# A style-modulated 1-D network as one convolution per sample: three of four samples by shared products instead of two

## The reference, cut to what matters

```
s = style @ mw.T + mb                       # per sample and input channel
weight = SCALE * w * s[:, None, :, None]
demod = rsqrt(sum(weight * weight, axis=(2, 3)) + EPS)
weight = weight * demod[:, :, None, None]   # per sample
out = x
for i, typ in enumerate(('same','upsample','same','downsample')):
    out = layer_i(out)                      # conv (and blur) with that sample's weight
return x + out
```

## Time and profile before

| | us |
|---|---|
| median of 3 runs (lowest to highest) | 675.08 (674.23 to 676.02) |
| the profiled execution | 674.02 |
| its span | 672.2 |
| TensorE busy | 660.9 |
| VectorE, GpSimd, ScalarE busy | 436.3, 366.1, 311.8 |

### The profile page before, as it was taken

How to read it: one execution, slowest core, us unless ns; L and a number is a source line. 1 busy time by engine, 2 the same in 40 slices (tenths; PEclk the granted TensorE clock), 3 DMA queues, 4 the chain that set the end, 5 groups by cost and what they waited for, 6 DMA issues and landing times.

```text
span 672.2 us, 12153 instructions
## 1 busy us (share of the span) xinstructions
PE 660.9 (98%) x4478; PEld 615.9 (92%) x4478; DVE 436.3 (65%) x648; ACT 311.8 (46%) x494; POOL 366.1 (54%) x387
## 2 busy tenths in 40 slices
PE   8998999999999999999999999999999999999987
PEld 7887999999999999999999999999999999999986
DVE  5996666867666665586675665665767766556551
ACT  4335454543544453544454454454454454455441
POOL 2447556566656556646556655546665555665410
PEclk9999999999999999999999999999999999999999
DMA  7238776567776667867657877657877666887763
GB/s 255 61 91 213 182 181 159 157 185 199 187 178 153 178 181 185 210 152 176 172 157 196 208 184 164 167 164 181 202 190 178 140 181 171 209 197 192 154 157 130
DMA packets 130603, 117.20 MB, mean 174 GB/s; under 512 B 6064, under 2 KB 97264, under 8 KB 130544
## 3 DMA queue, kind: packets, MB, share of 16 engines
q1 hardware_dynamic: 130176, 116.17, 68.7%
q10 hardware_dynamic: 368, 0.25, 0.2%
HBM read 36.51 MB, written 33.75 MB: 105 GB/s over the span
## 4 chain that ended last, share of the span: by engine, by line
PE 94%; DVE 4%; issue 1%; ACT 1%; POOL 0%; DVEq 0%; ACTq 0%; POOLq 0%
PE po L175 17%; PE po L176 17%; PE po L177 17%; PE pg L175 8%; PE pg L177 8%; PE pg L176 8%; PE pg L180 4%; PE pg L181 4%; PE pm L177 3%; PE pm L175 3%; PE pm L176 3%; PE pe L399 1%; PE pe L392 1%; PE pg L408 0%; PE pe L402 0%
## 5 line engine op out<-in xcount | busy, mean ns | idle before, releaser
L175 PE MATMUL po<-xh,W 128*128 128x256 f32 (+1 forms) x640 | 217.7, 340 | 2.8 <-DVE T L742 1.8
L176 PE MATMUL po<-xl,W 128*128 128x256 f32 (+1 forms) x640 | 217.0, 339 | 0.0
L177 PE MATMUL po<-xh,W 128*128 128x256 f32 (+1 forms) x640 | 216.8, 339 | 0.0
L177 PEld LDWEIGHTS po<-xh,W 128*128 128x128 f32 x640 | 125.6, 196 | 12.3
L175 PEld LDWEIGHTS po<-xh,W 128*128 128x128 f32 x640 | 125.0, 195 | 12.9 <-issue 3.3
L176 PEld LDWEIGHTS po<-xl,W 128*128 128x128 f32 x640 | 125.5, 196 | 9.9
L742 DVE SCALAR_TENSOR_TENSOR T<-po,DD,M 128x512 f32<-128x512 f32 x64 | 48.0, 750 | 97.1 <-PE po L177 64.3
L667 POOL TENSOR_TENSOR Q2l<-Q2f,Q2h 128x512 fp32r<-128x512 f32 x30 | 71.6, 2386 | 68.5 <-ACT Q2h L552 68.5
L733 DVE TENSOR_TENSOR xl<-X,xh 128x1032 fp32r<-128x1032 f32 x64 | 96.3, 1505 | 2.9 <-ACT xh L513 2.9
L513 ACT CAST xh<-X 128x1032 fp32r<-128x1032 f32 x64 | 80.9, 1265 | 37.2 <-PE po L177 36.1
L768 DVE TENSOR_TENSOR Wf<-pg,S 128x512 f32<-128x512 f32 x64 | 44.2, 691 | 77.2 <-PE pg L177 57.6
(11 more groups left out here) (174 smaller groups left out, 1483.3 us busy)
## 6 DMA issues: line engine op xcount, KB each, us to landing
X<-in_xin SPq DMA_DIRECT2D x64, 516.0 KB, 4.4
out<-T SPq DMA_DIRECT2D x64, 512.0 KB, 3.7
W<-W SPq DMA_DIRECT2D x93, 256.0 KB, 4.3
W<-W SPq DMA_DIRECT2D x31, 384.0 KB, 5.6
V<-V SPq DMA_DIRECT2D x32, 128.0 KB, 5.2
V<-W SPq DMA_DIRECT2D x32, 64.0 KB, 3.6
V<-Vx SPq DMA_DIRECT2D x32, 64.0 KB, 3.0
E<-in_ed SPq DMA_DIRECT2D x1, 768.0 KB, 7.4
```

Source lines behind the costliest of these rows:

```text
L175: eng.matmul(o, wh_, rh, start=first, stop=False)
L176: eng.matmul(o, wh_, rl, start=False, stop=False)
L177: return eng.matmul(o, wl_, rh, start=False, stop=last)
```

## The change

Sample 1 of each group is now computed by shared products too (`FFA = (1, 2, 3)`), so a group has one plain sample and three shared ones. What goes with it:

- `sums`, `sums_high`, `sums_low` and `cross_sums` work for both pairs of samples of a group: VectorE's sum has 768 elements instead of 384, the cast and the remainder 512 instead of 256, and the three DMAs are twice as large.
- GpSimd makes differences for sample 1 too, so even pairs are 1290 columns wide (`PW`) instead of 1032; odd pairs stay at 1548.
- VectorE's `t_out` now serves three samples of a group and ScalarE's only sample 0; ScalarE has three `m_out`.
- The scaling of Q3 (`q3_full`) goes from GpSimd (two instructions of 256 elements) to ScalarE (four of 128) from group 3 on.
- The hand-written orders of ScalarE, VectorE, GpSimd and SP are changed, within a group and in the first one. `sums` moves behind sample 1's `t_out`; SP stores an output pair ahead of `cross_sums`.
- The prologue ends after units 0 and 1 of group 1; units 2 and 3 of it come after sample 0. The 17 warm products in the middle become 22 right ahead of sample 0.

```
-PROLOGUE = [(0, u) for u in range(7)] + [(1, u) for u in range(4)]
+FFA = (1, 2, 3)
+PW = (2 * HW + XW, 2 * XW)
+WARM3 = 22
+PROLOGUE = [(0, u) for u in range(7)] + [(1, 0), (1, 1)]
 SLOTS = [[(2, 0), (2, 1)], [(1, 4), (1, 5), (1, 6)], [(2, 2)], [(2, 3)]]
+FIRST = {0: [[(1, 2), (1, 3)], [(2, 0), (2, 1)], [(1, 4), (1, 5), (1, 6)], [(2, 2)]],
+         1: [[(1, 3), (2, 0), (2, 1)]] + SLOTS[1:]}
...
 TensorE, conv(b):
-                if n % 2 == 0:
-                    if g:
-                        pe.wait_ge(s_tf, 2 * g - 1 + q)
+                def result_free():
+                    if b >= 2:
+                        if shared(b - 2):
+                            pe.wait_ge(s_tf, n_shared(b - 1))
+                        else:
+                            pe.wait_ge(s_td, n_plain(b - 1))
+                if not shared(b):
+                    result_free()
                     part(po[b % 2][:, :], (0, 1, 2, 3, 4), 0).then_inc(s_o, 1)
                     return
-                k = b // NG * 2 + q
+                k = n_shared(b)
...
                 if k:
                     pe.wait_ge(s_m, k)
                 part(pm[:, 0:256], (5, 6, 4), HW).then_inc(s_mm, 1)
-                pe.wait_ge(s_td, 2 * g + 1 + q)
+                result_free()
...
 SyncE:
                     cross(g + 1, 0)
                     cross(g + 1, 1)
+                store(n)
+                if g + 1 < NGR:
                     cross_sums(g + 1)
-                store(n)
...
 ScalarE:
+            def q3_full(g):
+                act.wait_ge(s_q3l, 2 * g)
+                for a in range(2):
+                    for i in range(2):
+                        b = g * NG + 2 * a + i
+                        m = act.activation(Q3f[:, a].rearrange("p v (o b) -> p (v o) b", b=2)[:, :, i],
+                                           q3s[:].rearrange("p v o -> p (v o)"), ACT.Copy, scale=D32[:, b:b + 1])
+                m.then_inc(s_q3f, 1)
...
 VectorE:
-                tt(Vf[:], Wf[:, 1, 0:3], Wf[:, 1, 1:4], ALU.add).then_inc(s_vf, 1)
+                tt(Vf[:], Wf[:, :, 0:3], Wf[:, :, 1:4], ALU.add).then_inc(s_vf, 1)
...
+                if b and shared(b - 1):
                     t_out(b - 1)
+                if weights_at(b - 1):
+                    sums(weights_at(b - 1))
                 for x in units_of(b):
                     full(*x)
...
                         w_low(x[0], 1)
-                        sums_low(x[0])
...
+                if weights_at(b - 1):
+                    sums_low(weights_at(b - 1))
+                if i == 2 and g + 1 < NGR:
+                    x_low(2 * g + 2)
```

More of the change, by code:

```diff
@@ L31, with shared, n_shared, n_plain @@
 EPS = 1e-8 * (C * 9)
-PROLOGUE = [(0, u) for u in range(7)] + [(1, u) for u in range(4)]
+WARM3 = 22
+PROLOGUE = [(0, u) for u in range(7)] + [(1, 0), (1, 1)]
 SLOTS = [[(2, 0), (2, 1)], [(1, 4), (1, 5), (1, 6)], [(2, 2)], [(2, 3)]]
+FIRST = {0: [[(1, 2), (1, 3)], [(2, 0), (2, 1)], [(1, 4), (1, 5), (1, 6)], [(2, 2)]],
+         1: [[(1, 3), (2, 0), (2, 1)]] + SLOTS[1:]}
+def shared(b):
+    return b % NG in FFA
+def n_shared(b):
+    return sum(shared(i) for i in range(b))
+def n_plain(b):
+    return b - n_shared(b)
 def units_of(b):
     g, i = divmod(b, NG)
-    return [(g + d, u) for d, u in SLOTS[i] if g + d < NGR]
+    return [(g + d, u) for d, u in FIRST.get(g, SLOTS)[i] if g + d < NGR]
+def weights_at(b):
+    return next((g for g, u in units_of(b) if u == 6), 0) if b >= 0 else 0
 ORDER = PROLOGUE + [x for b in range(B) for x in units_of(b)]
@@ L486, in constant @@
                 m.then_inc(s_pp, 1)
+            for x in PROLOGUE[4:7]:
+                unit(*x)
             constant(2, 1, SC_K2)
+            for x in PROLOGUE[7:]:
+                unit(*x)
+            constant(3, 3, SC_K3)
+            warm(WARM3, po[1])
             conv(0)
-            constant(3, 3, SC_K3)
             for b in range(B):
@@ L534, in t_out @@
                 act.wait_ge(s_o, b + 1)
-                if b % Q == 0 and n >= TR:
+                if n >= TR:
                     act.wait_ge(s_st[n % TR], 16 * (n // TR))
@@ L845, in edge, with final @@
                                              op0=ALU.add, op1=ALU.add).then_inc(s_ed, 1)
[L847 removed]
+            def final():
                 dve.wait_ge(s_pp, 7)
@@ L936, in _ @@
             reached(tt(tmp[lo, 3], kt[lo], S[lo, P3, :], ALU.mult))
-            g_low(1)
+            w_low(0, 1)
             sums(0)
+            full(1, 0)
+            full(1, 1)
             sums_low(0)
+            x_low(0)
+            q2_low(1)
+            final()
             for b in range(B):
                 g, i = divmod(b, NG)
-                if b == 1:
-                    constant()
-                if i in (3, 0) and b:
+                if b == 4:
+                    edges_begin()
+                if b and shared(b - 1):
                     t_out(b - 1)
+                if weights_at(b - 1):
+                    sums(weights_at(b - 1))
                 for x in units_of(b):
                     full(*x)
-                    if x[1] == 5:
-                        sums(x[0])
                     if x[1] == 6:
@@ L1028 @@
     r = run_bass_kernel_spmd(nc, [arrays], core_ids=[0])
-    o = r.results[0]["out_0"].reshape(B // 4, 2, 2, 2, C, L2).copy()
-    o[:, 1] = o[:, 1].reshape(B // 4, 2, 2, C, 2, L2 // 2).transpose(0, 1, 2, 3, 5, 4).reshape(B // 4, 2, 2, C, L2)
-    o = o.transpose(0, 1, 2, 4, 5, 3).reshape(B, C, L2, 2)
+    o = r.results[0]["out_0"].reshape(B // 4, 4, 2, C, L2).copy()
+    for i in FFA:
+        o[:, i] = o[:, i].reshape(B // 4, 2, C, 2, L2 // 2).transpose(0, 1, 2, 4, 3).reshape(B // 4, 2, C, L2)
+    o = o.transpose(0, 1, 3, 4, 2)
     o = o.reshape(B, C, 2 * L2)
```

198 lines of the change are left out of this document (116 added, 82 removed).

## The result

| | before | after |
|---|---|---|
| median (lowest to highest), 4 runs each | 675.14 (674.23 to 676.02) | 683.31 (682.41 to 684.07) |
| profiled execution, its span | 674.02, 672.2 | 683.69, 681.9 |
| TensorE, VectorE, GpSimd, ScalarE busy | 660.9, 436.3, 366.1, 311.8 | 653.8, 558.8, 456.9, 354.6 |

The change makes the kernel slower: ratio 1.0121, interval 1.0102 to 1.014. The forecast was 656.8 us and faster.

What follows compares the result with a forecast made beforehand. TensorE was taken as the bound. 18.3 (products) + 0.7 (start) - 0.3 (group 1 stall) - 0.3 (edges) - 0.15 (end) = 18.2 us off, giving a median of 656.8 us, range 653.5 to 660 (chance 0.70).

Steps and rivals of the forecast that it cites:

- The products: TensorE, sample 1 of each group: 3.49 to 2.90 us, group 19.45 to 18.86, 18.3 us off over groups 1 to 31.
- rival 3: TensorE: 256-column products cost more than half of 512-column ones, 0.4 us lost per group, 688 us; chance 0.01.
- Group 1's start: End of the prologue: group 1 begins at 58.7 instead of 59.38, bound by W's landing; 0.7 us gained.
- W's way through the DMAs: W lands 7.5 us after its last remainder, at about 37.1, wanted at 38.9: slack 1.8 us, nothing lost.
- rival 2: W's copies land late, way growing from 7.5 to 10.5 us, TensorE waits 1.2 us per group, 693 us; chance 0.05.
- ScalarE's busy time: Check on ScalarE across a group: its busy time should rise by about 1.5 us a group.
- sample 2's first product: TensorE: with one bank `pm`, it waits for sample 1's `M` on ScalarE; 1.5 us of slack, no stall.
- the chain between sample 2's product and the next sample 1's `M`: ScalarE and VectorE hand-offs: 12.8 us, then 3.1, ending at 29.2 against 30.7 wanted; slack 1.5 us, no stall.
- Rival 1: ScalarE and VectorE chain becomes the bound: 0.5 us late per group, 672 us; chance 0.09 in full, 0.13 for half.
- in steady groups the means are those used: Argument against VectorE's remainders running dearer: the chain's durations were the means seen in steady groups.
- Edges: Twelve groups with an edge step, VectorE held inside the chain: 0.3 us lost in all, up to 2.

Runs made afterwards that it cites:

- e6: e4 plus two waits, so GpSimd's remainders of units 1 and 2 wait for VectorE's odd and even `xl`: 668.03 us, 0.9877.
- e3: Changed kernel with GpSimd's odd-pair differences cut from 516 elements to 16 from pair 7 on (output wrong, timing only): 668.15 us, 0.9876.
- e4: Changed kernel with GpSimd's odd-pair differences moved behind the remainder of unit 2, nothing left out: 670.16 us, 0.9907.
- e10: Kernel before, with GpSimd's odd-pair differences moved from sample 2 to sample 1, as the change has them: 676.17 us, 1.0012.
- e5: Changed kernel with Q3's scaling put back on GpSimd and ScalarE's four activations gone: 689.7 us, 1.0202.
- e7: e6 plus GpSimd's scaled identities made earlier, behind unit 2's remainder, two groups ahead: 663.4 us, 0.9814.
- e1: Changed kernel with sample 1's `M` ahead of the cast of unit 6 in ScalarE's order: 684.13 us, 1.0116.
- e2: Changed kernel with a second bank for the shared products, taken from the units' four banks: 684.85 us, 1.0121.
- e8: e7 and e1 together, both edits in one kernel: 663.04 us, 0.9812.
- e9: e8 plus eight unread TensorE products ahead of the first product of group 1 and of group 31: 659.78 us, 0.9768.

## Why the prediction was wrong

**Right.** The products: 18.85 us in a quiet group, so the spacing of the Trainium skill ("TensorE: Matmul & The Clock Gate", Back-to-back issue gap) did not hold here and rival 3 is refuted. Group 1's start: 59.02 against 58.7; this is luck in part, since unit 5's copy began 0.65 us earlier than forecast (46.95) and the way from there to the end of W's remainders took 4.3 us instead of 3.5 (51.24). W's way through the DMAs: a copy lands in 5.6 us as before, and where TensorE waited for W, it got it 7.8 us (group 1) and 7.4 us (group 31) behind the last remainder, where it had been 7.5 and 7.4, so rival 2 is refuted too. ScalarE's busy time rose by 42.8 us, 1.3 a group; forecast 1.5. It was also right that the weak place is sample 2's first product, with ScalarE's `M` as releaser.

**The step that failed** is the chain between sample 2's product and the next sample 1's `M`, "12.8 us ... at 29.2 ... The slack is 1.5 us". It was summed from durations of the kernel before and from widths, in which VectorE had other neighbours. Every term with two SBUF operands was too small: `xl` 2.21 and 2.19 for 1.51 and 1.76, Vx 1.15 for 0.43, V 0.92 for 0.69, the addition 0.81 for 0.43, together 2.5 us. That is more than the slack of 1.5. The forecast's figures are what these instructions take alone (in e6 the even `xl` 1.50, V 0.69, Vx 0.42); what failed is that they were taken to be alone. VectorE's own loop, from `Vf` to `Vf`, which the forecast did not follow round, became 19.52 us; with the forecast's durations and W's remainders as in the kernel before it would be some 16.4 (an estimate). e3 and e4 show the cause: GpSimd's instructions alone were cut or moved, and 15 and 13 us came back. e10 shows it on two of the old kernel's durations, the sums and the addition, without any other part of the change; as these kept their shapes, width is not the reason. e5 shows the other sign. GpSimd's own queue is not the bound: in the changed kernel, e3 and e4 TensorE waits for GpSimd only once, 1.4 us in the prologue.

**Rival 1 was the case, and more of it**: I gave it 672 us, from one `xl` of 2.02, at 0.5 us in each of 30 groups. What came was 24.1 us of lateness in the middle groups, with a low clock behind waits (7 us between groups 1 and 31) that I had not counted. The row showed 1.25 to 2.02; I weighed its mean of 32 (1249) instead of asking which of GpSimd's instructions would stand beside the new order. The same trace had steadier signs, in every group (the kernel before, by form):

```profile
L667 POOL TENSOR_TENSOR Q2l<-Q2f,Q2h 128x512 fp32r<-128x512 f32 x30 | 71.6, 2386 | 68.5 <-ACT Q2h L552 68.5
...
L806 DVE TENSOR_TENSOR Vx<-Vf,Vx 64x128 fp32r<-64x128 f32 x32 | 21.7, 677 | 1.0
```

`Q2l`, begun inside the odd `xl`, takes 2386 ns where it takes 1.30 us alone (e6), and Vx took 677 ns beside GpSimd's `Q3l` at half the width for which I put 0.43 us. So "in steady groups the means are those used" did not hold for Vx. The Trainium skill ("SBUF — State Buffer", Who interferes with whom) has such VectorE instructions contend with GpSimd; the pairs above agree, on either engine's side (`xl` 2.48 us for 1.50, `ID` 2.02 for 0.61).

**A sum would have warned.** GpSimd's instructions of a group, undisturbed, are about 10.4 us in both kernels (two narrow differences came, Q3's scaling went); VectorE's with two SBUF operands grew from 6.3 to 7.4. If they exclude each other they take 17.8 of 18.85 us, where it was 16.7 of 19.45 (estimates from the shortest durations in these traces). In the room that is left VectorE must still do all its PSUM work in step with ScalarE. The sum is a warning and not the bound: e7 does the same instructions, and its quiet groups take 18.85 us.

**What the waits were.** That the bank `pm` or the place of the third `M` was at fault is refuted by e1, e2 and e8: removed, the waits came back at W. **Edges**: forecast 0.3 us in all, up to 2. The lateness that e4 leaves (10.7 us) stands in the edge groups and those behind them, 0.4 to 1.3 us in each, and e7 takes most of it away; in the changed kernel one of them takes 22.81 where e9 has 19.15. The term was too small in any order tried: even e9 keeps 3.1 us of lateness in the middle groups.

**Open.** Where the 3.0 us between e9 and the forecast of 656.8 are, of which lateness in the middle groups is 3.1 and the start 0.5 more, with gains elsewhere against them; and how a conflict splits between the two engines where neither is clearly first. In e7 GpSimd's second difference, begun at 305.72 and first held by the addition, ended only at 307.36, and W's remainder, begun at 306.18, passed it in 0.67 us, its length alone: the order of the starts is not the whole rule.

## What to carry to other kernels

When a change takes work off the bound engine, sum the helpers anew as if VectorE's instructions with two SBUF operands and all of GpSimd's ran one after the other, follow each helper's own loop round once, and lay both orders side by side before believing a slack of 1 or 2 us. A wait that vanishes from one place and comes back at another names a late loop, not a late instruction. Before giving up a change, move GpSimd's work under VectorE's PSUM instructions or make it wait for VectorE's wide ones: here that turned +1.2% into -1.9% (e7), and the unread products made it -2.3% (e9).

## What the runs showed of the hardware

- A VectorE instruction with two SBUF operands and one of GpSimd's that run side by side hold each other for nearly the whole instruction: `xl` of 1290 columns 1.50 us alone and 2.48 beside a `Gl`; `Vx` 0.42 and 1.21; GpSimd's `Q3h` of 64x256 0.74 (kernel before) and 1.94. VectorE's `T`, with one operand in PSUM, takes 742 ns in the changed kernel and 750 in the one before.
- Busy time of such engines says little: the same GpSimd instructions took 460.3 us in e4 and 385.6 in e6.
- Behind the wait of 2.24 us TensorE's granted clock fell to half, 1.2 of 2.4 GHz, and came back some 3 us later (changed kernel, two stretches, clock as the third number from the end):

```profile
315.00:318.00 3.00, 3.00 (x14) 3.00 (x15) 2.58 (x4) 1.79 (x3) 2.87 (x2) 0.52 0.68 132
318.60:322.00 3.40, 3.40 (x30) 3.40 (x29) 3.34 (x3) 0.53 (x2) 2.16 (x2) 1.00 1.11 205
```

Eight unread products in a wait of 2.0 and one of 2.7 us kept it at 1.00 (e9), 3.3 us for two places (3.0 by the ratios). Behind waits of 2.12 and 2.16 us in e3 and e4 it stayed at 1.00 without them.
